# Unscaled projections with GpSimd factors, spread chains, and 128-row low-rank products in a three-stage attention and expert kernel

## What is computed

```python
x = x + attn_a(layernorm(x))   # x is (2, 2048, 256); causal attention with a linear bias, 16 heads of 64
x = x + ffn(layernorm(x))      # x @ W_lin.T + b, plus 2 of 8 experts of rank 4, weighted by a softmax gate
x = x + attn_b(layernorm(x))   # hyperbolic attention, 16 heads of 16, 2048 tokens per batch entry
x = x + ffn(layernorm(x))      # the same weights again

# attn_b, with c and beta from two scalars:
q_h, k_h, v_h = exp_map_at_origin(q_t, c), ...      # v -> tanh(sqrt(c)|v|) / sqrt(c) * v / |v|, per token and head
arg  = max(1 + 2c |q-k|^2 / ((1 - c|q|^2)(1 - c|k|^2)), 1 + EPS)
w    = softmax(-beta * arccosh(arg) / sqrt(c))       # all 2048 keys, no mask
out  = log_map(exp_map(w @ log_map(v_h))) @ W_o.T
```

## Time and profile before

| | us |
|---|---|
| median of 3 runs | 5850.75 (5848.14 to 5853.64) |
| the profiled execution: its time | 5851.74 |
| the profiled execution: its span | 5849.9 |
| PE busy in the span | 4145.2 (71%) |
| DVE busy | 4754.5 (81%) |
| ACT busy | 4451.6 (76%) |
| POOL busy | 1446.9 (25%) |

### The profile page before, as it was taken

The page is one execution under the profiler, slowest core; times in us unless marked ns, Lnnn a source line. Parts: engine busy times, 40 slices in busy tenths (PEclk is TensorE's granted clock), DMA queues, the critical chain, the costliest instruction groups (busy, mean ns, idle before and its releaser), DMA issues. The chain is left out here.

```text
span 5849.9 us, 68952 instructions
## 1 busy us (share of the span) xinstructions
PE 4145.2 (71%) x22020; PEld 1848.0 (32%) x22020; DVE 4754.5 (81%) x7142; ACT 4451.6 (76%) x3412; POOL 1446.9 (25%) x1259
## 2 busy tenths in 40 slices
PE   8999999999999999645555555555555555555548
PEld 5555555555555555321111111111111111111105
DVE  7666666766666666669999999999999999999966
ACT  4555555555555555329999999999999999999993
POOL 0000000000000000134444444444444444444420
PEclk9999999999999999666667666666766676667667
DMA  1000000000000000158999999999999899999881
GB/s 39 5 5 5 5 5 6 4 8 5 5 6 5 5 2 1 35 151 178 192 195 189 195 189 195 189 195 189 195 187 194 185 197 186 198 186 198 185 183 62
DMA packets 149378, 637.95 MB, mean 109 GB/s; under 512 B 32662, under 2 KB 74840, under 8 KB 79064
## 3 DMA queue, kind: packets, MB, share of 16 engines
q0 software_dynamic: 73728, 536.90, 45.8%
q1 hardware_dynamic: 75224, 95.82, 4.9%
HBM read 69.46 MB, written 26.35 MB: 16 GB/s over the span
## 5 line engine op out<-in xcount | busy, mean ns | idle before, releaser
L1449 DVE SCALAR_TENSOR_TENSOR b_tiles<-b_ra_rep,b_cap,psum 128x1024 f32<-128x1024 f32 x1024 | 1261.5, 1272 | 67.6 <-PE psum L1719 60.8
L1719 PE MATMUL psum<-b_qT,b_kT 126*128 126x512 bf16 x2048 | 814.9, 509 | 696.7 <-DVE b_tiles L1449 693.5
L668 DVE CUSTOM_DVE_ANT_0 a_srow<-psum,a_bias 128x512 f32<-128x512 f32 (+3 forms) x1280 | 725.8, 607 | 497.4 <-PE psum L849 494.3
L727 ACT ACTIVATE a_pT<-psum 128x512 f32<-128x512 f32 (+3 forms) x1056 | 511.6, 527 | 661.0 <-PE psum L861 660.6
L1732 PE MATMUL psum<-b_tiles,b_v_aug 128*32 128x512 f32 x2752 | 524.8, 849 | 484.9 <-ACT b_tiles L1630 484.9
L1456 DVE TENSOR_SCALAR b_tiles<-b_tiles 128x2048 f32<-128x2048 f32 x512 | 775.3, 1514 | 4.3
L861 PE MATMUL psum<-ident,a_srow 128*128 128x128 f32 x4352 | 625.8, 281 | 70.5 <-DVE a_pT L541 32.9
L1622 ACT ACTIVATE b_tiles<-b_tiles 128x4096 f32<-128x4096 f32 x172 | 613.1, 3611 | 35.4 <-DVE b_tiles L1092 34.5
L745 ACT ACTIVATE a_srow<-a_srow,a_nmax 128x1536 f32<-128x1536 f32 (+15 forms) x512 | 610.3, 1197 | 23.2 <-DVE a_nmax L674 21.3
L1719 PEld LDWEIGHTS psum<-b_qT,b_kT 126*128 126x128 bf16 x2048 | 156.9, 110 | 1486.7 <-DVE b_tiles L1449 1126.4
L849 PE MATMUL psum<-a_k,a_q 64*128 64x512 f32 (+3 forms) x2560 | 624.6, 573 | 0.0
(11 more groups left out here) (215 smaller groups left out, 5326.1 us busy)
## 6 DMA issues: line engine op xcount, KB each, us to landing
b_tiles<-b_tiles POOLq DMA_DIRECT2D x344, 1024.0 KB, 13.2
X<-b_tiles POOLq DMA_DIRECT2D x168, 1024.0 KB, 13.3
b_ra_rep<-ra_scratch SPq DMA_DIRECT2D x32, 1024.0 KB, 10.0
row_scratch<-b_tiles SPq DMA_DIRECT2D x6, 2048.0 KB, 14.0
b_qk_raw<-row_scratch SPq DMA_DIRECT2D x31, 288.0 KB, 2.9
X<-in_x_dram SPq DMA_DIRECT2D x8, 512.0 KB, 6.7
a_wqk<-in_wqk_dram SPq DMA_DIRECT2D x32, 128.0 KB, 2.7
x_scratch<-X SPq DMA_DIRECT2D x4, 1024.0 KB, 10.7
```

Source lines behind the costliest of these rows:

```text
L668: nc.vector.tensor_tensor_reduce(out=srow[:, n % ROWS, h, a:z], in0=bank(c % 2 * 2 + h, 0, z - a), in1=bias[:, h, off + a:off + z], scale= ...
L1449: nc.vector.scalar_tensor_tensor(out=a[:, s * HALF:(s + 1) * HALF], in0=ra_rep[:, j, s * HALF:(s + 1) * HALF], scalar=cap[:, j, k:k + 1], ...
L1719: last = nc.tensor.matmul(half_ps(s)[:, i * BANK:(i + 1) * BANK], kT[:, j, k * P:(k + 1) * P], qT[:, j, cs], start=True, stop=True)
```

## The change

1. *Low-rank products.* `ra`, `tl` and `tlT` grow from 33 to 128 rows (or columns), and what is added is zero. POOL zeroes `ra` before it is loaded (`zero`), and the 95 extra columns of `tl` at the start of each expert stage.
2. *Unscaled rows.* `scale(b)` is gone. q, k and v are stored as projected, with seven factors per head and token tile in place of four (`F_Q`, `F_K`, `F_V` are new). `prepare` and `take_v` multiply by the factors on POOL as they copy a head.
3. *Chains.* `scalars_of` and `factors(0)` are cut into pieces that stand between normalizations of later tiles; the square root and the tanh of b = 0 come one and two groups later; of `factors(1)` two pieces follow the copies of head 0.
4. *Main loop.* The first batches hold two chunks instead of four, and weights are as wide as their batch. POOL squares from chunk 2 on. SP stores the rows of b = 1 without waiting for POOL, v first, and `first_use` waits for less.
5. SP waits for the weights of the projection before it stores `X`.

```diff
 class Experts:
-        self.ra = ctx.enter_context(nc.sbuf_tensor(f"{name}_ra", [E * R + 1, D], F32))
+        self.ra = ctx.enter_context(nc.sbuf_tensor(f"{name}_ra", [P, D], F32))
+    def zero(self):
+        self.nc.gpsimd.memset(self.ra[:, :], 0.0).then_inc(self.zeroed, 1)
 ...
-        tl = sb("tl", [P, NT, RA])
-        tlT = sb("tlT", [RA, 2, 4 * P])
+        tl = sb("tl", [P, NT, P])
+        tlT = sb("tlT", [P, 2, 4 * P])
 ...
+            pool.memset(tl[:, :, RA:P], 0.0).then_inc(ones_done, 1)
 ...
-ROOTS, KEPT = 4, 4
-WIDE, WIDE_W = 2, 4
+ROOTS = [2] * 4 + [4] * ((CHUNKS - 8) // 4)
+WIDE = 2
 ...
-            return SQUARES[c % len(SQUARES)] if c >= NO_POOL else "D"
+            return SQUARES[c % len(SQUARES)]
 ...
-                step(engine.tensor_copy(aug[:, 0, :, 0:DB], rows(0)))
+                step(engine.tensor_tensor(aug[:, 0, :, 0:DB], rows(0), each(F_Q), ALU.mult))
 ...
-            engine.tensor_copy(v_aug[:, g % 2, :, 0:DB], v).then_inc(S["v_ready"], 1)
+            engine.tensor_tensor(v_aug[:, g % 2, :, 0:DB], v, f.unsqueeze(2).to_broadcast([P, TB, DB]), ALU.mult
+                                 ).then_inc(S["v_ready"], 1)
 ...
             sp.dma_start(w_in, w_qkv.rearrange("(c p) n -> p c n", p=P)).then_inc(S["w_loaded"], 16)
+            sp.wait_ge(S["w_loaded"], 16)
 ...
+            sp.wait_ge(S["tok_copied"], TB)
+            for i in range(3):
+                store_row(0, i, S["row_saved0"])
+            store_factors(0)
 ...
+            sp.wait_ge(S["tok_copied"], NT)
+            store_row(1, 2, S["v_saved1"])
+            for i in range(2):
+                store_row(1, i, S["row_saved1"])
+            store_factors(1)
 ...
-            scale(0)
-            pool.wait_ge(S["tok_scaled"], 3)
+            pool.wait_ge(S["factors_done"], 1)
+            pool.wait_ge(S["tok_copied"], TB)
             for part in range(3):
                 prepare(pool, nc.gpsimd, 0, part)
 ...
-            scale(1)
 ...
-                if n == 11:
-                    scalars_of()
-                if n == TB + 4:
-                    factors(0)
+                if n in (6, 10, 14, 18):
+                    scalars_of((n - 6) // 4)
+                if n == TB + 7:
+                    lengths(0)
+                if n in (TB + 12, TB + 14, TB + 16):
+                    factors(0, (n - TB - 12) // 2)
 ...
-            factors(BATCH - 1)
+            factors(BATCH - 1, 0)
             for i in range(4):
                 group_copied(0, i)
+            for part in (1, 2):
+                factors(BATCH - 1, part)
 ...
+                if 1 <= q <= 3:
+                    scalars_of(q - 1)
+                if q == TB // 4 + 1:
+                    roots_all(0)
+                if q == TB // 4 + 2:
+                    tanhs(0)
 ...
-            for a, z in root_batches:
+            for n, (a, z) in enumerate(root_batches):
                 for c in range(a, z, WIDE):
                     root(c)
-                upto = z - KEPT if z < CHUNKS else CHUNKS
-                if upto > weighted:
+                if n:
                     nc.scalar.preload_act_table_set("natural_log_exp_and_others")
-                for c in range(weighted, upto, WIDE_W):
-                    weight(c)
+                    weights(n - 1)
```

More of the change, by code:

```diff
@@ L166, in _ @@
         def _(pool):
+            if out is not None:
+                experts.zero()
             for j in range(E):
@@ L999, in stage_attn_b @@
         sc = sb("sc", [P, 24])
-        NS_Q, E_K, EN_K, CAP_K = range(4)
+        NS_Q, E_K, EN_K, CAP_K, F_Q, F_K, F_V = range(7)
         NF = TB * HB
@@ L1092, in square_by @@
             engine.tensor_tensor(y_slot(c), a, a, ALU.mult).then_inc(S["sq_" + name], 1)
-        root_batches = [(c, min(c + ROOTS, CHUNKS)) for c in range(0, CHUNKS, ROOTS)]
+        root_batches = [(sum(ROOTS[:n]), sum(ROOTS[:n + 1])) for n in range(len(ROOTS))]
+        assert root_batches[-1][1] == CHUNKS
         PREP = 17
@@ L1111, in of, with each @@
                 return f.unsqueeze(2)
+            def each(i):
+                return of(i).to_broadcast([P, TB, DB])
             def rows(i):
@@ L1137, in prepare @@
                 step(engine.tensor_copy(aug[:, 1, :, DB + 1:AUG], of(EN_K)))
-                step(engine.tensor_copy(aug[:, 1, :, 0:DB], rows(1)))
+                step(engine.tensor_tensor(aug[:, 1, :, 0:DB], rows(1), each(F_K), ALU.mult))
                 sync()
@@ L1216, in store_o, with store_row, store_factors @@
                 sp.dma_start(o_scratch[:, g * ROW_K:(g + 1) * ROW_K], o_raw[:, :]).then_inc(S["o_stored"], 16)
-            for b in range(BATCH):
+            def store_row(b, i, saved):
+                hs = slice(b * HB, (b + 1) * HB)
+                at = (0, ROW_K, ROW - ROW_K)[i]
+                sp.dma_start(rows[:, hs, at:at + ROW_K], tok[b][:, i, :, :, :].rearrange("p h t d -> p h (t d)")
+                             ).then_inc(saved, 16)
+            def store_factors(b):
                 hs = slice(b * HB, (b + 1) * HB)
@@ L1263, in _ @@
                 sp.wait_ge(x_back[q], 16)
-            for b in range(BATCH):
-                sp.wait_ge(S[f"row_saved{b}"], 64)
         @block.gpsimd
@@ L1551, in _, with scalars_of @@
             norm.roots(act, 0, NT)
[L1553 to L1562 removed]
+            T = 11
+            def scalars_of(part):
+                if part == 0:
+                    act.wait_ge(S["gz_done"], 1)
+                    nc.scalar.activation(col(T + 2, 2), col(T, 2), ACT.Exp).then_inc(S["scal"], 1)
+                    act.wait_ge(S["scal"], 1)
+                    nc.scalar.activation(col(T + 4, 2), col(T + 2, 2), ACT.Ln, bias=col(ONE)).then_inc(S["scal"], 1)
+                elif part == 1:
+                    act.wait_ge(S["gz_done"], 2)
+                    nc.scalar.activation(col(SC), col(C), ACT.Sqrt).then_inc(S["scal"], 1)
+                else:
+                    act.wait_ge(S["gz_done"], 3)
+                    nc.scalar.activation(col(T + 9), col(T + 7), ACT.Ln).then_inc(S["scal"], 1)
             def roots_all(b):
@@ L1707, in _ @@
             pe.wait_ge(S["grp_copied"], 4)
+            ra_transposes(BATCH - 1)
             pe.wait_ge(S["tok_copied"], NT)
```

263 lines of the change are left out of this document (123 added, 140 removed).

## The result

| | before | after |
|---|---|---|
| median of 4 runs, us | 5850.81 (5848.14 to 5853.64) | 5780.64 (5779.47 to 5783.76) |
| ratio, 95% interval | | 0.9881 (0.9864 to 0.9898) |
| profiled span, us | 5849.9 | 5777.7 |
| granted clock of the profiled execution, mean | 0.813 | 0.819 |

What follows compares the result with a forecast made beforehand. ACT is full in the steady loop, so gains lie in the expert stages, projection and loop's start: -4.3 - 10.9 - 1 - 28.2 + 1 - 27.4 = -70.8 us, giving a median of 5780 (55%), range 5762 to 5807.

Steps and rivals of the forecast that it cites:

- Clock: Low-rank products, both expert stages: filled rows, zeros included, keep PE's clock up; 64 products give back 13.8 us of PE.
- Rival A: Expert stages: zero rows don't count for the clock, the gains are lost and the memsets stay; 5801 us, 20%.
- First expert stage: ffn0: DVE becomes the limit, so -6.9 us from the products and +2.6 for the memset, -4.3 in all.
- The zeroing: Expert stages' opening: POOL's new memset holds DVE's layernorm operation until it ends, +2.6 us in ffn0 and +2.9 in ffn1.
- rival C: Expert stages' opening: the memset holds nothing; 5775 us, 15%.
- Weights: Projection's second group: with SP's new wait the weight load runs alone, -1 us (0 to -1.9).
- Projection: Group copies: 52.8 us falls to 14.7, the next groups cost +12.0, then 0 to the last tile; sum -28.2 us.
- Loop's start: Main loop's first chunks: ACT's roots and weights, counted from the first argument, come sooner, 98 us for 125.4, -27.4.
- the 4.1 for the sums: Loop's start: ACT's idle time before the first Ln, which waits for the sums until 33.0 us.
- Loop: Steady main loop: POOL's added products in prepare and take_v cost 0 us (to +5 over the loop).
- rival D: Main loop: prepare's products on POOL make ACT wait at each head; slower past 2.4 us a head, 5870 at 3; 2%.
- Rival B: Projection and loop's start: gains half given back, -20 and -18 us for -28.2 and -27.4; 5798 us, 8%.

Runs made afterwards that it cites:

- a1_narrow: Changed kernel with the low-rank operands back at 33 rows and no zeroing of the extra columns; median 5800.0 us, ratio to before 0.9914.
- a2_fill: Kernel before with only the fill of the low-rank operands to 128 rows (item 1); median 5830.8 us, ratio 0.9970.
- a3_rows: Changed kernel with 128 rows only in the products' operands, transposes writing 33 rows, 1024 columns zeroed once for 3040; median 5781.3 us, ratio 0.9882.
- b1_best: Changed kernel joining a3_rows, q1_between and batches of four from the start, its memset waiting for four normalized tiles; median 5764.1 us, ratio 0.9851.
- q1_between: Changed kernel with the three factor pieces of b = 0 behind the sums of tiles 20, 24 and 26; median 5774.9 us, ratio 0.9870.
- s2_wide: Changed kernel with three useless 4096-column GpSimd products where the scaling of b = 1 stood; median 5794.9 us, ratio 0.9907.

## Why the prediction was right, and where its sizes were off

- **Clock**: right. 128 rows, zeros included, give 1.00, and 33 rows 0.50, both ways round (a1_narrow, a2_fill). Rival A is dead. The size was short: I counted the 64 products (13.8, measured 13.1) and left out the 32 transposes, which ran at half clock too and gave back 2.7 us of PE. With the hold of 2.5 put back the last stage won 16.1, not 13.8.
- **First expert stage**: DVE as the new limit held, -4.8 for -4.3.
- **The zeroing**: right in mechanism and size (2.3 and 2.5 us held, 2.6 and 2.9 said); rival C is dead (a3_rows, b1_best).
- **Weights**: the second group copy came after 3.17 us for 3.84, -0.7 for -1. a2_fill, which lacks SP's new wait, took 3.66.
- **Projection**: the 52.8 us became 13.9 (14.7 said), and the two groups behind took 10.7 more (12.0 said): the two pieces ahead of the last normalization did cost their whole length. My 0 from there to the last tile was wrong: the clock was low through the start of the group, 24.6 for 22.2 us. Most of the cost was a matter of place, not of work: 16.2 us for 26.4 in q1_between, 13.9 without pieces. From the last tile to the first argument it was +1.6 for +1.
- **Loop's start**: -23.9 for -27.4. The mis-sized step is "then squares chunk 2 to 24.0; root of 2, 3 to 27.6". I had POOL's DMAs and square in a row, but not that POOL's square takes 4.24 us there for 3.6 and that DVE's square of chunk 3, begun under it, waits for its end (5.92 us for 2.3): it was ready at 27.0. Hence 8.11 us of wait for 5.3, and 4.39 more at chunk 10. Against that the 4.1 for the sums did not appear. That the scaling was the main cause is shown (16.7 of 23.9, s2_wide), though by the length of one operation rather than, as I had it, by that and the DMAs behind it.
- **Loop**: no idle time added (0.9 us ahead of a whole group, as before), rival D is dead. Rival B's half loss did not come.
- **Luck**: the -3.1 us of the first stage is scatter, two short falls of the clock that before's profile has and after's has not; it hid about as much as the loop's start was missed by (3.5). And the last stage's extra 2.7 made up for the projection's missing 1.7. That the total came within 1 us of the forecast owes something to both.

The Trainium skill, "TensorE: Matmul & The Clock Gate", "Why this matters for your kernels", has a K=32 matmul take as long as a K=128 one. At the same clock this case's traces agree: 377 ns with 33 rows and 384 with 128. In a stretch where TensorE does little else the narrow ones ran at 0.50 and took 640 ns (a1_narrow), so the rule alone gives the wrong time there.

## What to carry to other kernels

Look at the granted clock of a stretch in which TensorE is busy with narrow operands; if it is 0.5, fill the contraction rows with zeros, once, and only on the product's operand; 64 rows were enough here. Put GpSimd's long operations where VectorE rests, or cut them short: count the longest one, not their sum. Put a helper chain between two steps whose consumer has a buffer to spare, not ahead of the step that everyone waits for.

## What the runs showed that I had not expected

64 rows of 128 keep the clock at 1.00 where 33 bring it to 0.50. At 1.00 a product with 33 rows is as quick as one with 128 (377 and 384 ns). A GpSimd memset of zeros holds VectorE's operation until it ends (2.46 us under 2.63), and a square of VectorE's that begins under one of GpSimd's takes 5.92 us for 2.3, ending its own length after the other. The first attention stage, alike in all kernels, scatters by 6 us (0.26%) between profiled executions, and the longer ones have two short falls of the clock; what brings these about stays open.
